# Two-bank order of TensorE's products in a graph-network kernel: first layer, and the second way's second layer

## The chip, the cores and the metric

The kernel runs on one core of one Trainium2 chip. The metric is device microseconds of the whole program, the median of three runs. One further execution was profiled; every duration below comes from it.

## The reference, cut to what matters

A graph with 3,125 nodes of 128 features and 53,125 edges passes through two blocks, each followed by a residual addition and a layer norm. The first block is where the change lies. For every edge an MLP of three layers (384 to 256 to 256 to 128) runs twice, once on (from, to, edge) and once on (to, from, edge), and the results are summed at the target node:

```
def _prop_once(node_states, f_idx, t_idx, edge_features, w1, b1, w2, b2, w3, b3):
    edge_inputs = jnp.concatenate([node_states[f_idx], node_states[t_idx], edge_features], axis=1)
    x = relu(edge_inputs @ w1.T + b1)
    x = relu(x @ w2.T + b2)
    return segment_sum(x @ w3.T + b3, t_idx)
agg = _prop_once(x, src, dst, ...) + _prop_once(x, dst, src, ...)
```

Three GRU cells then use `agg`; the second block is three layers of neighbour sums with a two-layer MLP each.

## The kernel before, in words

The edges are cut into G = 104 groups of GE = 512. `edge_stage` handles one group per turn; `gru_stage` and `sum_stage` follow it. Within `edge_stage` each engine has a `turn(g, ...)` of its own, and the order of its work is written out by hand. The engines meet only at semaphores (`pe.wait_ge(s_he, ...)` and the like). PSUM has eight banks of 128x512 fp32, used by number. Products are made in fp32r with each operand split into a high and a low part, so a product with a 128-wide contraction is three matmuls: high x high, low x high, high x low.

TensorE's turn for group g (L1370) is, in this order:

- `upright(g, 0)` (matmuls at L1329 and L1333): the first way's second layer for the first half of the edges, into bank 6.
- `turn_sd(g + 1)` (L1231, L1310, L1311) and `pairs_of(g)` (L1345): node features of the next group, and edge counts of this one.
- `upright(g, 1)` (L1329, L1333): the other half of the edges, into bank 7.
- `turn_e(g + 1)` (L1231): four 128x128 transposes of the next group's edge features.
- `second(g, 2)` and `second(g, 3)` (L1283): the second way's second layer. Each is six matmuls of 512 columns, the first into bank 6, the other into bank 7.
- `first(g + 1)` (L1270): the first layer of the next group, 18 matmuls of 512 columns. For f = 0 and 1 it makes a shared part (six matmuls, bank 2 + 2f, signalled by `s_p`) and a part whose sign differs between the ways (three matmuls, bank 3 + 2f, signalled by `s_q`).
- `third(1)` (L1293) and `total(g)` (L1361, L1366): the third layer of the second way, and the sums at the nodes.

ScalarE's turn (L707) has in this order: a copy (L624), `upright(g, 0)` (L675, reads bank 6 into `he`), the cast L629, `upright(g, 1)` (L675, reads bank 7 into `he` and raises `s_he` to 2g + 2), the cast L637, `second(g, 2)` and `second(g, 3)` (L667, which read banks 6 and 7 after `s_l2`), the cast L643, in three turns of four a `clear` (L704), then `first(g + 1)`: `shared(0)` (L648, waits for `s_p`), `hidden(0, 0)` (L653), `shared(1)`, and three more `hidden`; then `results` (L682, the tile `es`) and `sums` (L698).

VectorE's `ways(g + 1)` (both at L898, rest at L902) turns the first layer's two parts into `hpre` and `h1l`. It waits for the output of L648 and for `s_q`. Eight times in the whole run a turn ends with `wrap` (L1036, L1038).

`second(g, 2)` writes over bank 6 and `second(g, 3)` over bank 7, so each must wait until ScalarE's L675 has read what `upright` left there. In the kernel before, the first waits for `s_he` at 2g + 1 and the second for 2g + 2.

Of the kernel before, what the change touches and what calls it, by code (L numbers as in the profile page):

```python
# [34 lines left out]
HB = H // P  # L35
# [3 lines left out]
GE = K * P  # L39
# [54 lines left out]
def edge_stage(nc, block, seam, a, adj_flat, tables, along, degrees, npairs, aggw, later, taken, tabs):  # L94

    ctx = ExitStack()
    with ctx:
        def sb(name, shape, dt=fp32):
            return ctx.enter_context(nc.sbuf_tensor(name, shape, dt))

        sem = seam.sem
        bank = seam.bank
# [4 lines left out]
        w1h = sb("w1h", [P, HB, 3, P], f32r)  # L107
        w1l = sb("w1l", [P, HB, 3, P], f32r)
# [31 lines left out]
        sdl = sb("sdl", [P, 3, GE], f32r)  # L140
# [23 lines left out]
        sdh = sb("sdh", [P, 3, GE], f32r)  # L164
# [79 lines left out]
        s_lo = sem("s_lo")  # L244
# [4 lines left out]
        s_p = sem("s_p")  # L249
        s_q = sem("s_q")  # L250
# [4 lines left out]
        s_l2 = sem("s_l2")  # L255
        s_h2 = sem("s_h2")
        s_l3 = sem("s_l3")
        s_he = sem("s_he")
# [970 lines left out]
        def _(pe):  # L1229
            def transpose(out, in_, n):  # L1230
                return nc.tensor.transpose(out, in_, ident[0:n, 0:n])  # L1231
# [3 lines left out]
            for s in range(2):  # L1235
                for k in range(K):
                    last = transpose(bank[s][:, k * G:(k + 1) * G],
                                     rows_f[:, s, :].rearrange("g (p k) -> g k p", k=K)[:, k, :], G)
# [9 lines left out]
            for f in range(HB):  # L1248
                for k in range(HB):
                    last = transpose(bank[4][:, (k * HB + f) * P:(k * HB + f + 1) * P],  # L1250
                                     w2n[:, f, k * P:(k + 1) * P], P)
            last.then_inc(s_wT, 1)
            for k in range(HB):
                last = transpose(bank[5][:, k * P:(k + 1) * P], w3n[k], P)
# [4 lines left out]
            def first(g, start=False, pairs=False):  # L1259
                if not start:  # L1260
                    pe.wait_ge(s_hp, g * 4)
                for f in range(HB):
                    if pairs and f == 1:
                        pe.wait_ge(s_acc, g * 2)
                    for bk, signal, js in ((2, s_p, (0, 2)), (3, s_q, (1,))):
                        parts = [(w, j, x) for j in js for w, x in ((w1h, sdh), (w1h, sdl), (w1l, sdh))]
                        for q, (w, j, x) in enumerate(parts):
                            if f == 0 and j == 2 and q == 3:
                                pe.wait_ge(s_lo, g * 2 + 2)
                            last = nc.tensor.matmul(bank[bk + 2 * f][:, :], w[:, f, j, :], x[:, j, :],  # L1270
                                                    start=(q == 0), stop=(q == len(parts) - 1))
                        last.then_inc(signal, 1)

            PARTS2 = [(w, k, h) for k in range(HB) for w, h in ((w2h, "h"), (w2h, "l"), (w2l, "h"))]

            def units_of(h, way, k, lo, hi):
                return h1h[:, way, k, lo:hi] if h == "h" else h1l[:, k, way, lo:hi]

            def second(g, n):

                way, f = divmod(n, HB)
                for q, (w, k, h) in enumerate(PARTS2):
                    last = nc.tensor.matmul(bank[6 + f][:, :], w[:, k, f, :], units_of(h, way, k, 0, GE),  # L1283
                                            start=(q == 0), stop=(q == len(PARTS2) - 1))
                last.then_inc(s_l2, 1)
# [13 lines left out]
            def windowed():  # L1299
                def turn_sd(g, par, turns, start=False):  # L1300
                    if not start:
                        pe.wait_ge(s_agg, g - 1)
                        pe.wait_ge(s_out, g - 1)
                    pe.wait_ge(s_x[par], turns * (K * 16) + K * 16)
                    for k in range(K):
                        last = transpose(bank[0][:, k * P:(k + 1) * P], xg[par][:, k, :], P)
                    last.then_inc(s_sdT, 1)
                    pe.wait_ge(s_hot, g + 1)
                    pe.wait_ge(s_xl, g + 1)
                    nc.tensor.matmul(bank[1][:, :], xwh[0:SPAN, :], hot[0:SPAN, :], start=True, stop=False)  # L1310
                    nc.tensor.matmul(bank[1][:, :], xwl[0:SPAN, :], hot[0:SPAN, :], start=False, stop=True).then_inc(s_sdT, 1)  # L1311

                def turn_e(g, par, turns, extra=0):
                    pe.wait_ge(s_xs, g + 1)
                    pe.wait_ge(s_ef[par], turns * 16 + (16 + extra))
                    for k in range(K):
                        last = transpose(bank[0][:, k * P:(k + 1) * P], ef[par][:, k, :], P)
                    last.then_inc(s_eT, 1)

                def upright(g, n):  # L1320

                    if n == 0:
                        pe.wait_ge(s_h1l, g * 4 + 4)
                    if not (isinstance(g, int) and g == 0):
                        if n == 0:
                            pe.wait_ge(s_h2, g * 2 - 1)
                        else:
                            pe.wait_ge(s_es, g)
                    nc.tensor.matmul(bank[6 + n][:, :], ones_r[:, :], b2hl[:, :, :].rearrange("p t u -> p (t u)"),  # L1329
                                     start=True, stop=False)  # L1330
                    for t in range(2 * n, 2 * n + 2):
                        for q, (w, k, h) in enumerate(PARTS2):
                            last = nc.tensor.matmul(bank[6 + n][:, t % 2 * H:(t % 2 + 1) * H],  # L1333
                                                    units_of(h, 0, k, t * P, (t + 1) * P),
                                                    w[:, k, :, :].rearrange("p f m -> p (f m)"),
                                                    start=False,
                                                    stop=(q == len(PARTS2) - 1 and t % 2 == 1))
                    last.then_inc(s_l2, 1)

                def pairs_of(g):  # L1340

                    pe.wait_ge(s_ah, g + 1)
                    for half in range(2):
                        for t in range(2):
                            last = nc.tensor.matmul(bank[4 + half][:, 0:WIDER], rowhot[:, half * 2 + t, :],  # L1345
                                                    colhot[:, half * 2 + t, :], start=(t == 0), stop=(t == 1))
                        last.then_inc(s_aT, 1)

                def pair_keys():
                    pe.wait_ge(s_spots, 1)  # L1350
                    for j in range(2):
                        for t in range(K):
                            last = transpose(bank[4 + j][:, t * G:(t + 1) * G],
                                             outb[j][0:G, t, :], G)
                    last.then_inc(s_akT, 1)
# [14 lines left out]
                def turn(g, par, turns, ahead=2, extra=0):  # L1370
                    begin = isinstance(g, int) and g == 0
                    upright(g, 0)
                    if ahead:
                        turn_sd(g + 1, 1 - par, turns)
                    if begin:
                        pair_keys()
                    else:
                        pairs_of(g)
                    upright(g, 1)
                    if ahead:  # L1380
                        turn_e(g + 1, 1 - par, turns, extra)
                    for n in range(2, 4):
                        pe.wait_ge(s_he, g * 2 + (n - 1))
                        second(g, n)
                    if begin:
                        pairs_of(g)
                    if ahead:
                        pe.wait_ge(s_lo, (g + 1) * 2 + 1)
                        first(g + 1, pairs=True)
                    if not ahead:  # L1390
                        into_each()
                        pe.wait_ge(s_agg, g)
                    pe.wait_ge(s_h2, g * 2 + 2)
                    third(1)
                    total(g, par)
# [28 lines left out]
                turn_e(0, 0, 0)  # L1424
                pe.wait_ge(s_lo, 1)
                first(0, start=True)
                turn(0, 0, 0)
                turn(1, 1, 1)
                with pe.Fori(1, (G - 2) // 2) as i:
                    turn(i * 2, 0, i)  # L1430
                    turn(i * 2 + 1, 1, i + 1)
# [127 lines left out]
class Seam:  # L1559
# [20 lines left out]
    def sem(self, name):  # L1580
        return self.ctx.enter_context(self.nc.semaphore(name))
# [748 lines left out]
```

## Time and profile before

| | |
|---|---|
| median of 3 runs | 2269.28 us (2268.61 to 2270.14) |
| the profiled execution | 2266.19 us |
| its span | 2264.4 us |
| PE (TensorE matmul) busy | 2210.4 us, 98% |
| DVE (VectorE) busy | 1777.3 us, 78% |
| ACT (ScalarE) busy | 1166.0 us, 51% |
| POOL (GpSimd) busy | 1165.7 us, 51% |
| mean granted TensorE clock | 0.995 |

The span runs from the first to the last instruction, and 1.8 us of the execution lie around it. PE's busy time counts a matmul from its start to its modelled end, and neighbours overlap in it. What a matmul costs in a stream is therefore the distance between two starts. A row of the timeline gives start, duration, engine, line, operation and count, and in brackets the idle time before it with the releaser. The edge stage fills the span from 37 to 1836 us.

### The profile page before, as it was taken

What the parts mean: (1) busy time and instruction counts of PE and PEld (TensorE: products, weight loads), DVE (VectorE), ACT (ScalarE), POOL (GpSimd) and SP (SyncE); (2) the same over time, 40 slices, a digit from 0 to 9 for tenths busy, and PEclk for the clock granted to TensorE, in tenths of its full rate; (3) what the DMA queues carried; (4) which work ended last, traced back from release to release, by engine and by line L of the source; (5) the groups of instructions that cost most, each with busy time, mean ns of one, the idle gap of its engine ahead of it and who ended that gap; (6) DMA issues with size and microseconds to landing.
All of it is one profiled execution on the core that took longest, in us unless ns stands there. A gap on an engine that the chain in (4) does not pass through costs nothing.

```text
span 2264.4 us, 39847 instructions
## 1 busy us (share of the span) xinstructions
PE 2210.4 (98%) x13211; PEld 1845.9 (82%) x13211; DVE 1777.3 (78%) x4138; ACT 1166.0 (51%) x2019; POOL 1165.7 (51%) x858
## 2 busy tenths in 40 slices
PE   4999999999999999999999999999999999899998
PEld 3888888888888888888888888888888864587876
DVE  7888898898889889888988988898899836703112
ACT  4555566556565555555655565555565533411122
POOL 2466666666666666666666666666665640001100
PEclk9999999999999999999999999999999999999999
DMA  4357455455445445544544544554454359186965
GB/s 154 68 114 149 92 111 99 90 111 108 92 93 115 93 101 110 100 90 101 108 101 93 116 94 90 116 102 91 100 110 92 58 99 271 57 353 258 397 261 209
DMA packets 242868, 292.67 MB, mean 129 GB/s; under 512 B 126820, under 2 KB 200375, under 8 KB 234704
## 3 DMA queue, kind: packets, MB, share of 16 engines
q1 hardware_dynamic: 169554, 237.15, 33.4%
q0 software_dynamic: 73216, 54.58, 18.9%
q14 instruction: 81, 0.66, 0.1%
q8 instruction: 17, 0.28, 0.1%
HBM read 218.56 MB, written 73.08 MB: 129 GB/s over the span
## 4 chain that ended last, share of the span: by engine, by line
PE 94%; DMA 2%; DVE 2%; issue 1%; POOL 1%; ACT 1%; POOLq 0%; SPq 0%; DVEq 0%; ACTq 0%
PE bank L1270 19%; PE bank L1333 13%; PE bank L1283 12%; PE bank L2229 9%; PE bank L1293 8%; PE bank L1361 8%; PE bank L1366 4%; PE bank L1345 4%; PE bank L1231 4%; PE bank L1329 2%; PE bank L1881 2%; PE bank L1310 2%; PE bank L1889 1%; DMA l_ring<-adj 1%; PE bank L1311 1%
## 5 line engine op out<-in xcount | busy, mean ns | idle before, releaser
L514 POOL DMA_INDIRECT sums<-outb,target x416 | 662.2, 1592 | 551.3 <-ACT outb L698 440.4
L507 POOL DMA_INDIRECT xg<-in_x,gidx x416 | 477.4, 1148 | 150.3 <-issue 141.7
L653 ACT ACTIVATE h1h<-hpre 128x512 fp32r<-128x512 f32 x416 | 257.8, 628 | 131.0 <-DVE hpre L898 130.7
L902 DVE SCALAR_TENSOR_TENSOR h1l<-hpre,h1h 128x512 fp32r<-128x512 f32 x416 | 268.6, 688 | 17.0 <-ACT h1h L653 17.0
L898 DVE TENSOR_TENSOR hpre<-pb,bank 128x512 f32<-128x512 f32 x416 | 265.7, 679 | 4.2 <-ACT pb L648 3.4
L1270 PE MATMUL bank<-sdh,w1h 128*128 128x512 f32 x624 | 246.8, 395 | 3.4 <-DVE sdl L930 2.7
L1270 PE MATMUL bank<-sdh,w1l 128*128 128x512 f32 x624 | 247.7, 397 | 0.0
L1270 PE MATMUL bank<-sdl,w1h 128*128 128x512 f32 x624 | 244.8, 392 | 0.0
L1333 PE MATMUL bank<-w2h,h1l 128*128 128x256 f32 x832 | 234.0, 281 | 0.0
L1333 PE MATMUL bank<-w2l,h1h 128*128 128x256 f32 x832 | 233.6, 281 | 0.0
L1333 PE MATMUL bank<-w2h,h1h 128*128 128x256 f32 x832 | 233.3, 280 | 0.0
L667 ACT ACTIVATE h<-bank,b2c 128x512 f32<-128x512 f32 x208 | 143.6, 691 | 145.7 <-PE bank L1283 145.7
L1293 PEld LDWEIGHTS bank<-w3t,h 128*128 128x128 f32 x1664 | 201.7, 192 | 9.3 <-issue 0.2
L1293 PE MATMUL bank<-w3t,h 128*128 128x128 f32 x1664 | 202.5, 275 | 0.1
L1361 PE MATMUL bank<-into,h 128*128 128x64 f32 x1664 | 197.3, 272 | 0.0
L1361 PEld LDWEIGHTS bank<-into,h 128*128 128x128 f32 x1664 | 194.2, 192 | 0.0
L1283 PE MATMUL bank<-h1h,w2h 128*128 128x512 f32 x416 | 172.2, 414 | 0.0
L1016 DVE TENSOR_SCALAR colhot<-spots,colkey 128x475 bf16<-128x475 f16 x416 | 168.4, 405 | 0.0
L2109 DVE TENSOR_TENSOR l_xl<-l_xb,l_xh 128x128 fp32r<-128x128 f32 (+1 forms) x75 | 21.0, 289 | 185.4 <-ACT l_xh L2054 185.4
L1333 PEld LDWEIGHTS bank<-w2h,h1l 128*128 128x128 f32 x832 | 157.6, 189 | 9.2
L629 ACT CAST sdh<-sd 128x1024 fp32r<-128x1024 f32 x104 | 109.1, 1049 | 107.7 <-DVE sd L921 107.7
L1283 PE MATMUL bank<-h1h,w2l 128*128 128x512 f32 x416 | 163.0, 392 | 0.0
(282 smaller groups left out, 4706.7 us busy)
## 6 DMA issues: line engine op xcount, KB each, us to landing
l_ring<-adj SPq DMA_DIRECT2D x54, 1568.0 KB, 7.7
rowb<-along SPq DMA_DIRECT2D x104, 512.0 KB, 4.3
ef<-in_edge_attr SPq DMA_DIRECT2D x103, 256.0 KB, 2.8
adj<-band SPq DMA_DIRECT2D x46, 480.0 KB
adj<-band SPq DMA_DIRECT2D x23, 540.0 KB
stay<-adj SPq DMA_DIRECT2D x6, 1568.0 KB, 15.0
xg<-in_x,gidx POOLq DMA_INDIRECT x416
sums<-outb,target POOLq DMA_INDIRECT x416, 4.1
```

What stands on the lines that cost most here:

```text
L507: pool.indirect_dma_start(out=to, out_offset=None, in_=a["x"], in_offset=bass.IndirectOffsetOnAxis(ap=ids, axis=0)).then_inc(s_x[par], 16)
L514: pool.indirect_dma_start(out=tables[k % 2], out_offset=bass.IndirectOffsetOnAxis(ap=target[par][:, 1, k:k + 1], axis=0), in_=outb[par][:, ...
L653: nc.scalar.activation(h1h[:, way, f, :], hpre[:, f, way, :], ACT.Relu).then_inc(s_h1, 1)
L898: nc.vector.tensor_tensor(hpre[:, f, way, :], pb[:, f, :], bank[3 + 2 * f][:, :], op).then_inc(s_hp, 1)
L902: nc.vector.scalar_tensor_tensor(out=h1l[:, f, way, :], in0=hpre[:, f, way, :], scalar=0.0, in1=h1h[:, way, f, :].bitcast(fp32), op0=ALU.m ...
L1016: nc.vector.tensor_scalar(colhot[:, t, 0:WIDE], spots[:, 0:WIDE], of(colkey, t), None, ALU.is_equal)
L1270: last = nc.tensor.matmul(bank[bk + 2 * f][:, :], w[:, f, j, :], x[:, j, :], start=(q == 0), stop=(q == len(parts) - 1))
L1283: last = nc.tensor.matmul(bank[6 + f][:, :], w[:, k, f, :], units_of(h, way, k, 0, GE), start=(q == 0), stop=(q == len(PARTS2) - 1))
L1293: last = nc.tensor.matmul(bank[6 + way][:, t * P:(t + 1) * P], h2[:, way, k, t * P:(t + 1) * P], w3t[:, k, :], start=not bias and k == 0, ...
L1333: last = nc.tensor.matmul(bank[6 + n][:, t % 2 * H:(t % 2 + 1) * H], units_of(h, 0, k, t * P, (t + 1) * P), w[:, k, :, :].rearrange("p f m ...
L1361: last = nc.tensor.matmul(bank[0][:, k * SPAN:(k + 1) * SPAN], he[:, t, k * P:(k + 1) * P], into[par][:, t, :], start=(t == 0), stop=(t == ...
L2229: last = nc.tensor.matmul(lane(n)[:, 0:width(n)], part[0:r, :], cols if exact else cols.bitcast(fp32), start=False, stop=end)
```

## The change

In `first` the matmuls of the two parts are interleaved: six that go to banks 2 + 2f and 3 + 2f by turns, then the remaining three of the shared part to bank 2 + 2f. `s_q` is raised after the sixth, `s_p` after the ninth. The wait for `s_lo` (2g + 2) stands ahead of the seventh matmul, where it stood ahead of the fourth. In TensorE's windowed `turn` the two calls of `second` are replaced by one loop of twelve matmuls that go to banks 6 and 7 by turns. One wait, for `s_he` at 2g + 2, stands ahead of all twelve. `s_l2` is raised after the eleventh and after the twelfth; it was raised after the sixth and the twelfth. Number, shapes and operands of the matmuls stay the same.

```diff
--- before.py
+++ after.py
@@ -1262,14 +1262,17 @@
                 for f in range(HB):
                     if pairs and f == 1:
                         pe.wait_ge(s_acc, g * 2)
-                    for bk, signal, js in ((2, s_p, (0, 2)), (3, s_q, (1,))):
-                        parts = [(w, j, x) for j in js for w, x in ((w1h, sdh), (w1h, sdl), (w1l, sdh))]
-                        for q, (w, j, x) in enumerate(parts):
-                            if f == 0 and j == 2 and q == 3:
-                                pe.wait_ge(s_lo, g * 2 + 2)
-                            last = nc.tensor.matmul(bank[bk + 2 * f][:, :], w[:, f, j, :], x[:, j, :],
-                                                    start=(q == 0), stop=(q == len(parts) - 1))
-                        last.then_inc(signal, 1)
+
+                    parts = [(j, w, x) for w, x in ((w1h, sdh), (w1h, sdl), (w1l, sdh)) for j in (0, 1)]
+                    parts += [(2, w, x) for w, x in ((w1h, sdh), (w1h, sdl), (w1l, sdh))]
+                    for q, (j, w, x) in enumerate(parts):
+                        if f == 0 and q == 6:
+                            pe.wait_ge(s_lo, g * 2 + 2)
+                        done = nc.tensor.matmul(bank[(3 if j == 1 else 2) + 2 * f][:, :], w[:, f, j, :], x[:, j, :],
+                                                start=q < 2, stop=q in (5, 8))
+                        if q == 5:
+                            done.then_inc(s_q, 1)
+                    done.then_inc(s_p, 1)
 
             PARTS2 = [(w, k, h) for k in range(HB) for w, h in ((w2h, "h"), (w2h, "l"), (w2l, "h"))]
 
@@ -1379,9 +1382,13 @@
                     upright(g, 1)
                     if ahead:
                         turn_e(g + 1, 1 - par, turns, extra)
-                    for n in range(2, 4):
-                        pe.wait_ge(s_he, g * 2 + (n - 1))
-                        second(g, n)
+                    pe.wait_ge(s_he, g * 2 + 2)
+                    for q, (w, k, h) in enumerate(PARTS2):
+                        for f in range(HB):
+                            last = nc.tensor.matmul(bank[6 + f][:, :], w[:, k, f, :], units_of(h, 1, k, 0, GE),
+                                                    start=(q == 0), stop=(q == len(PARTS2) - 1))
+                            if q == len(PARTS2) - 1:
+                                last.then_inc(s_l2, 1)
                     if begin:
                         pairs_of(g)
                     if ahead:
```

## Rows read from the trace of the kernel before

**Rows 1.** Page: busy time by engine; the chain that ended last, by line.
```profile
PE 2210.4 (98%) x13211; PEld 1845.9 (82%) x13211; DVE 1777.3 (78%) x4138; ACT 1166.0 (51%) x2019; POOL 1165.7 (51%) x858
...
PE bank L1270 19%; PE bank L1333 13%; PE bank L1283 12%; PE bank L2229 9%; PE bank L1293 8%; PE bank L1361 8%; PE bank L1366 4%; PE bank L1345 4%; PE bank L1231 4%; PE bank L1329 2%; PE bank L1881 2%; PE bank L1310 2%; PE bank L1889 1%; DMA
```

**Rows 2.** Waits, PE alone, 100 to 1800 us: us in total, times, longest.
```profile
PE bank L1231 <- DMA xg<-in_x,gidx: 0.6, 2, 0.5
```

**Rows 3.** Chain in order of time, one turn: start, us, what.
```profile
1020.47 0.44 PE bank L1231 x4
1020.90 2.76 PE bank L1283 x12
1023.66 4.16 PE bank L1270 x18
```

**Rows 4.** Timeline at `upright(g, 1)` and `second(g, 2)`, turns at 76, 1020 and 1329 us.
```profile
76.69 0.60 ACT L675 ACTIVATE h<-bank 128x512 f32<-128x512 f32 x1
...
76.85 0.48 PE L1283 MATMUL bank<-h1h,w2h 128*128 128x512 f32 x1
...
1020.19 0.28 PE L1333 MATMUL bank<-w2l,h1h 128*128 128x256 f32 x1
...
1020.66 0.48 PE L1283 MATMUL bank<-h1h,w2h 128*128 128x512 f32 x1
...
1020.50 0.60 ACT L675 ACTIVATE h<-bank 128x512 f32<-128x512 f32 x1
...
1329.59 0.60 ACT L675 ACTIVATE h<-bank 128x512 f32<-128x512 f32 x1 [0.15 <-PE bank L1333]
...
1329.75 0.48 PE L1283 MATMUL bank<-h1h,w2h 128*128 128x512 f32 x1
```

**Rows 5.** Timeline: a wait of PE that did last, turn 0.
```profile
62.44 0.65 DVE L1030 TENSOR_TENSOR band<-band,bank 128x475 f32 x1
...
63.15 0.50 PE L1270 MATMUL bank<-sdh,w1h 128*128 128x512 f32 x1 [0.62 <-DVE band L1030]
```

**Rows 6.** A turn after `wrap` at 1295 us, and how many there are.
```profile
1295.38 0.59 ACT L675 ACTIVATE h<-bank 128x512 f32<-128x512 f32 x1
...
1295.12 0.48 PE L1283 MATMUL bank<-h1h,w2h 128*128 128x512 f32 x1
...
L1036 DVE TENSOR_TENSOR band<-band x8: 646/646/651, 259.7 to 1701.1; 128x475 f32<-128x475 f32 x8
```

**Rows 7.** Timeline, PE: L2229, L1345; last, L1345 grouped: busy, mean ns.
```profile
2002.48 1.66 PE L2229 MATMUL bank<-l_ring,l_xh 128*128 128x512 f32 x7
2003.98 1.66 PE L2229 MATMUL bank<-l_ring,l_xl 128*128 128x512 f32 x7
...
1017.81 1.02 PE L1345 MATMUL bank<-colhot,rowhot 128*128 128x500 bf16 x4
...
L1345 PE MATMUL bank<-colhot,rowhot 128*128 128x500 bf16 x416 | 106.1, 377 | 0.0
```

**Rows 8.** Timeline, one turn: ACT, then DVE and PE behind the first layer.
```profile
1008.22 0.68 ACT L648 ACTIVATE pb<-bank,b1c 128x512 f32<-128x512 f32 x1
...
1013.11 0.57 ACT L682 COPY es<-bank 128x512 f32<-128x512 f32 x1
...
1008.20 0.39 PE L1270 MATMUL bank<-sdh,w1l 128*128 128x512 f32 x1
...
1010.27 0.40 PE L1270 MATMUL bank<-sdh,w1l 128*128 128x512 f32 x1
...
1014.03 1.11 PE L1366 MATMUL bank<-es,same 128*128 128x128 f32 x8
...
1009.22 1.27 DVE L898 TENSOR_TENSOR hpre<-pb,bank 128x512 f32<-128x512 f32 x2
...
1011.26 1.28 DVE L898 TENSOR_TENSOR hpre<-pb,bank 128x512 f32<-128x512 f32 x2
```

## The prediction

> **What bounds the kernel now.** I read the page first. PE is busy for 98% of the span and the chain that ended last runs almost wholly through it; the two line numbers that the change touches, L1270 and L1283, hold 19% and 12% of that chain [rows 1]. The other engines have room. Then the waits of PE in the edge stage: between 100 and 1800 us it waited 0.6 us in total for anybody [rows 2]. So a turn of this stage is the sum of PE's own instructions. A saving on them shortens it, and a wait that PE has to sit out lengthens it, one for one. The chain in order of time gives the pieces of a turn without the overlap of neighbours: the twelve matmuls of `second` last 2.76 us, 230 ns each; the eighteen of `first` 4.16 us, 231 ns each; the four transposes between `upright(g, 1)` and `second` only 0.44 us [rows 3]. A turn lasts 17.15 us, and there are 104.
>
> Times are compared so: my sum is made against the profiled execution (2266.19 us, of it 2264.4 the span). The median of the three runs, 2269.28, is 3.1 us above it, and the same increase is laid on it. A difference under 0.2%, 4.5 us, is about what a measurement of this kernel cannot tell from no change.
>
> **The changed order itself.** Count, shapes and operands stay. What changes is how often a matmul goes to another bank than the one before it. In `first`, 14 of the 17 steps between its matmuls stay in their bank before and 4 after; in `second`, 10 of 11 before and none after. That is 20 steps more per turn into another bank, 2080 in all. Is such a step cheaper? The trace has a stretch where every step is of this kind: the second block's panels (L2229) send seven matmuls to seven banks in rotation, six of 512 columns and one of 64. The seven take 2003.98 - 2002.48 = 1.50 us [rows 7]. Give the 64-column one 0.11 us, what one of the transposes of similar weight load takes (0.44 / 4, [rows 3]), and a 512-column matmul costs (1.50 - 0.11) / 6 = 232 ns. In the same bank it is 230 or 231 [rows 3]. Type and width agree (fp32r, 512). Other things differ (L2229 keeps one weight tile for seven matmuls, and rings are loading beside it), but a saving that belongs to the bank should show there and does not. I take zero.
>
> The bounds of this term: above, 2 ns more on each of 2080 steps, +4 us. Below, the bf16 matmuls of L1345 step (1.02 - 0.38) / 3 = 214 ns for 500 columns (0.38 us being the mean length of one, 377 ns), so 219 ns for 512 [rows 7]: 11.5 ns less on 2080 steps, -24 us. I stay at the L2229 end because type and width are the same there; bf16 shows that the engine can do better with other data, not with other banks, as each pair of those matmuls stays in one bank.
>
> Beside it a page. The Trainium skill (TensorE: Matmul & The Clock Gate, section Back-to-back issue gap) puts the isolated gap at N / 2.4 + 2.5 ns, 216 ns for 512 columns. No row of an fp32r matmul here reaches it. Were the bank the reason for the 14 ns between it and the 230 in the trace, 2080 steps would give back 30 us.
>
> **The wait that moved.** This is the term that counts. Before the change the six matmuls into bank 6 start while ScalarE still reads bank 7; only the second six need that bank, 1.4 us later. After it, the one wait for `s_he` at 2g + 2 stands ahead of the first matmul, and the second matmul needs bank 7 in any case. ScalarE's read of bank 7 (L675) cannot start until `upright(g, 1)` is done, and does so at once: the last L1333 ends at 1020.19 + 0.28 = 1020.47, L675 starts at 1020.50 and takes 0.60 us, to 1021.10 [rows 4]. PE has only its 0.44 us of transposes to put in between, and today starts L1283 at 1020.66 [rows 4]. How fast does PE go on after a wait? In turn 0 one did last: VectorE ends at 62.44 + 0.65 = 63.09, the matmul starts at 63.15, 0.06 later [rows 5]. So the first L1283 would start at 1021.10 + 0.06 = 1021.16 and not at 1020.66: 0.50 us. The turn at 76 us gives 76.69 + 0.60 + 0.06 - 76.85 = 0.50, the one at 1329 us 1329.59 + 0.60 + 0.06 - 1329.75 = 0.50 [rows 4]. They are the first and the last of 18 ordinary turns that I read; all give 0.50 or 0.51. Nothing shifts with it in its favour: transposes and L675 both hang on the same end of `upright(g, 1)`, so the gap reappears in each turn.
>
> Two kinds of turn cost more. After a `wrap`, of which there are eight, VectorE and with it ScalarE's cast are late, and L675 ends at 1295.38 + 0.59 = 1295.97, against a first L1283 at 1295.12: 0.91 us with the release [rows 6]. In the last turn there are no transposes, so nothing covers the 0.44 us that they do elsewhere: 0.50 + 0.44 = 0.94 us. Sum: 95 x 0.50 + 8 x 0.91 + 0.94 = 47.5 + 7.3 + 0.9 = 55.7 us.
>
> What is queued behind the waiting PE: `second`, `first(g + 1)`, `third`, `total`, the whole rest of the turn. It all moves by the same amount.
>
> On one page the Trainium skill speaks against this order: Perfetto Trace Analysis, section Matmuls, has independent groups rotate through the banks so that the emptying of one bank runs beside the next group's matmuls. Before, that is what happens at L675 and bank 6; the trace agrees, L1283 starting at 1020.66 in the midst of L675 [rows 4]. By that rule the time comes out on the same side as mine.
>
> **The signals that moved.** `s_q` comes three matmuls earlier, which releases nobody, since VectorE waits for L648 as well. `s_p` comes three later, 0.69 us. For f = 0 it now falls at the end of the ninth matmul, 1008.20 + 0.39 = 1008.59; L648 ran at 1008.22 [rows 8]. With PE's own 0.50 it starts near 1009.13 and ends near 1009.81. VectorE was busy with other work until 1009.22 [rows 8], and that work hangs on the turn before, so L898 starts 0.62 us later than now, 0.12 more than PE has moved. For f = 1 the signal is the end of the last matmul, 1010.27 + 0.40 + 0.50 = 1011.17; L648 (0.67) ends near 1011.88, L898 starts near 1011.91 instead of 1011.26, a lag of 0.15 against PE. The two L667, now released one matmul apart, end about 0.4 us later against PE; `clear` and the new release of L648 fall together, no more is added. The lag goes down to `es` (L682). Today it ends at 1013.11 + 0.57 = 1013.68 and L1366 starts at 1014.03 [rows 8]: 0.35 us, less 0.06 for the release leaves 0.29. A lag of 0.15 fits in. Cost: nothing; if that cover were gone, the lag would be paid in every turn, 0.15 x 103 = 15 us. The other wait moved in `first` (`s_lo`) stands later than before, so it can only be met sooner.
>
> **Sum.** 55.7 us: the profiled execution would go to 2321.9, the median to 2269.3 + 55.7 = 2325.0.
>
> **The rivals.**
>
> 1. The alternation shortens a matmul, beside the stall. With the bf16 step of 219 ns: 2325 - 24 = 2301. Against it L2229. At the floor of one column per cycle of 2.4 GHz (the mean granted clock is 0.995 of full speed), 213 ns, the 20 changed steps give 17 x 2080 = 36 us: 2289. Chance 0.06.
>
> 2. The other side, not slower: the bank sets the step for all thirty matmuls, also those that stay in their bank, and all fall to that floor. 30 x 104 = 3120 matmuls by 17 ns, 54 us, against 56: 2271, the same. It decides from 16.4 ns per matmul on (51.2 us / 3120), which leaves a step of 214 ns. Against it: no fp32r row is near. Chance 0.02; faster by over 0.2% needs still more, or a stall that is hidden by something I don't see: 0.01 of this.
>
> 3. The first layer's chain on ScalarE and VectorE becomes late. If `s_p` carried its full three matmuls down to `es`, 0.69 - 0.29 = 0.40 us in 103 turns, 41 us: 2366. For it: the chain L648, L898, L653, L902 has little slack at its end. Against it: VectorE's own work covers the first 0.5 us. Chance 0.08, mostly of a part of it.
>
> 4. The change doesn't do what it says: the wait bites only at the first matmul that writes bank 7, so one matmul passes, 0.23 us less in each turn, 24 us: 2301. Against it: the diff puts the wait ahead of the loop. Chance 0.02.
>
> **How the numbers follow.** My forecast keeps 0.82. Its own spread: the release 0.02 us longer or shorter (2 us), steps up to 2 ns longer (+4), a remainder of the lag (+5), and a few ns of gain at each changed step (7 ns is -15). That gives 2310 to 2337, and rivals 1, 3 and 4 lie mostly outside, with 0.16. Slower by over 0.2%: 0.82 + 0.05 + 0.08 + 0.02 = 0.97, the case in rival 1 included; same 0.02; faster 0.01.
>
> **What would show it.** In the profile after: a wait of PE, L1283 for ScalarE's L675, about 104 times and 0.4 to 0.5 us each, where there was none; the turn 17.65 instead of 17.15 us; L1283 x12 and L1270 x18 in the chain still at 230 ns a matmul; both L667 back to back; L1366 without a wait for L682. I am wrong if L1283's wait is missing or covered, if the step within L1270 is 220 ns or less, or if PE waits at L1366 or L1329 too.

## Result, and the profile after

| | before | after |
|---|---|---|
| median | 2268.95 us (4 runs, 2268.54 to 2270.14) | 2327.21 us (4 runs, 2325.58 to 2330.67) |
| ratio, 95% interval | | 1.0263 [1.025, 1.0276] |
| profiled execution, of it the span | 2266.19, 2264.4 us | 2327.14, 2325.4 us |
| PE busy | 2210.4 us, 98% | 2239.8 us, 96% |
| a turn in the edge stage | 17.15 us | 17.68 us |

The change costs 58.3 us, 2.6%. The forecast was 2325.0 us, within 2310 and 2337.

The waits of PE between 100 and 1850 us, to be held against [rows 2] (waiting line and releaser, us in total, times, longest):

```profile
PE bank L1388 <- ACT h L675: 29.0, 98, 0.8
PE bank L1231 <- DMA xg<-in_x,gidx: 0.4, 1, 0.4
```

L1388 is the new loop of twelve matmuls. A wait that did not exist stands in each of the 98 turns of this window, and no other has come. The 29.0 us are less than the loss, because this view counts idle time from the modelled end of the last transpose, which overlaps its successor elsewhere; it shows 0.30 us a turn where the prediction had announced 0.4 to 0.5. The chain in order of time (the chain of work that ended last, followed back from its end) counts without overlap (start, us, what), to be held against [rows 3]:

```profile
1052.08 1.42 PE bank L1336 x12
1053.50 0.02 issue
1053.52 0.60 ACT h L675
1054.12 0.04 issue
1054.17 3.04 PE bank L1388 x12
1057.21 4.16 PE bank L1271 x18
1061.37 1.78 PE bank L1296 x16
1063.15 1.73 PE bank L1364 x16
1064.89 0.95 PE bank L1369 x8
```

The chain now leaves PE once a turn. After the last matmul of `upright(g, 1)` it runs through ScalarE's L675 and comes back; the four transposes are no longer on it. From the end of `upright(g, 1)` to the end of `second` it was 1023.66 - 1020.47 = 3.19 us [rows 3] and is 1057.21 - 1053.50 = 3.71 us: 0.52 more. The eighteen matmuls of `first` last 4.16 us, as before.

The same place in the timeline (start, duration, engine, line, and in brackets the idle time and its releaser), with ScalarE and VectorE behind the first layer, to be held against [rows 4, 8]:

```profile
1053.52 0.60 ACT L675 ACTIVATE h<-bank 128x512 f32<-128x512 f32 x1 [0.15 <-PE bank L1336]
...
1054.17 0.74 PE L1388 MATMUL bank<-h1h,w2h 128*128 128x512 f32 x2 [0.25 <-ACT h L675]
1054.75 0.61 PE L1388 MATMUL bank<-h1l,w2h 128*128 128x512 f32 x2
1055.20 0.62 PE L1388 MATMUL bank<-h1h,w2l 128*128 128x512 f32 x2
1055.66 0.62 PE L1388 MATMUL bank<-h1h,w2h 128*128 128x512 f32 x2
...
1041.50 0.28 DVE L925 TENSOR_TENSOR xwl<-xw,xwh 64x128 fp32r<-64x128 f32 x1
1042.37 1.29 DVE L898 TENSOR_TENSOR hpre<-pb,bank 128x512 f32<-128x512 f32 x2 [0.60 <-ACT pb L648]
...
1046.30 0.57 ACT L682 COPY es<-bank 128x512 f32<-128x512 f32 x1
...
1047.04 1.11 PE L1369 MATMUL bank<-es,same 128*128 128x128 f32 x8
```

L675 ends at 1054.12 and the first pair of matmuls starts 0.05 us later. From then on each pair takes 0.45 to 0.47 us, 230 ns per matmul, with every step into the other bank. VectorE, which was busy almost right up to L898 before (4.2 us of idle time ahead of it in the whole run, now 90.9), is free early and waits 0.60 us for L648. `es` ends at 1046.87 and L1369 starts at 1047.04, 0.17 us behind it.

The turn after a `wrap`:

```profile
273.00 1.05 ACT L629 CAST sdh<-sd 128x1024 fp32r<-128x1024 f32 x1 [1.76 <-DVE sd L921]
273.96 0.59 ACT L675 ACTIVATE h<-bank 128x512 f32<-128x512 f32 x1
...
274.60 0.74 PE L1388 MATMUL bank<-h1h,w2h 128*128 128x512 f32 x2 [0.80 <-ACT h L675]
```

Here ScalarE's cast is late and sets L675. From the starts of `second` in neighbouring turns, the eight turns of this kind are 18.22 or 18.23 us long, 1.07 more than an ordinary turn of before. In the last turn `second` starts 0.88 us later against its neighbour than it did. The sum in the trace: 95 x 0.525 + 8 x 1.07 + 0.88 = 59.3 of the 61.0 us between the two spans. Most of the rest, 1.6 us, lies in turn 0, where TensorE's granted clock differed between the two executions (next view: turn 0 from one start of `second` to the next; after the length come PE's busy time and count, then the granted clock; before, then after).

```profile
56.56:76.85 20.29, 18.47 (x118) 1.00 0.18 48
...
56.53:78.94 22.41, 20.30 (x115) 0.92 0.16 43
```

PE stands idle for 1.2 us in this turn, ahead of its last sums. In the execution of after, the clock then was at its lower level, 1.2 GHz, from 70.4 to 73.7 us (0.50 in that stretch): L1369's eight matmuls last 1.96 us and not the 1.16 of before, and those of L1336 step 0.21 us and not 0.12. The change is not the reason. Of the nine profiled executions in this document, turn 0 has a clock of 0.92 in four, two of them without the stall, and lasts 22.1 to 22.4 us; it has 1.00 in five and lasts 20.3 to 21.3 us. Why the same idle time is followed by the lower clock in only four of them is open.

```profile
70.20 1.96 PE L1369 MATMUL bank<-es,same 128*128 128x128 f32 x8 [1.22 <-ACT es L682]
...
72.60 0.41 PE L1336 MATMUL bank<-w2h,h1l 128*128 128x256 f32 x1
72.81 0.41 PE L1336 MATMUL bank<-w2l,h1h 128*128 128x256 f32 x1
```

### The profile page after: what moved, and what is told of

Same layout as the page of the kernel before. It is cut to its first block, busy times and chain, and to the rows that moved or that the text cites. A ratio compares the mean times of both kernels' runs of the same rounds, so it can differ in the third digit from the quotient of the medians.

```text
span 2325.4 us, 39797 instructions
## 1 busy us (share of the span) xinstructions
PE 2239.8 (96%) x13211; PEld 1850.2 (80%) x13211; DVE 1777.6 (76%) x4138; ACT 1161.4 (50%) x2019; POOL 1179.6 (51%) x858
## 4 chain that ended last, share of the span: by engine, by line
PE 86%; DVE 5%; ACT 5%; issue 2%; DMA 1%; POOL 0%; DVEq 0%; POOLq 0%; SPq 0%; ACTq 0%
PE bank L1271 17%; PE bank L1388 13%; PE bank L1336 11%; PE bank L2236 9%; PE bank L1296 7%; PE bank L1364 7%; PE bank L1369 4%; PE bank L1348 4%; ACT h L675 3%; PE bank L1888 2%; PE bank L1332 2%; PE bank L1231 2%; PE bank L1313 2%; PE bank L1896 1%; PE bank L1314 1%
## 5 line engine op out<-in xcount | busy, mean ns | idle before, releaser
L507 POOL DMA_INDIRECT xg<-in_x,gidx x416 | 490.1, 1178 | 150.6 <-issue 141.6
L898 DVE TENSOR_TENSOR hpre<-pb,bank 128x512 f32<-128x512 f32 x416 | 267.1, 683 | 90.9 <-ACT pb L648 90.9
L667 ACT ACTIVATE h<-bank,b2c 128x512 f32<-128x512 f32 x208 | 131.6, 685 | 252.7 <-PE bank L1388 252.7
L1336 PE MATMUL bank<-w2h,h1l 128*128 128x256 f32 x832 | 233.8, 281 | 0.0
L1336 PE MATMUL bank<-w2l,h1h 128*128 128x256 f32 x832 | 233.8, 281 | 0.0
L1336 PE MATMUL bank<-w2h,h1h 128*128 128x256 f32 x832 | 233.3, 280 | 0.0
L1271 PE MATMUL bank<-sdh,w1h 128*128 128x512 f32 x624 | 214.8, 398 | 3.4 <-DVE sdl L930 2.7
L1271 PE MATMUL bank<-sdh,w1l 128*128 128x512 f32 x624 | 212.0, 394 | 0.0
L1271 PE MATMUL bank<-sdl,w1h 128*128 128x512 f32 x624 | 211.7, 393 | 0.0
L1388 PE MATMUL bank<-h1h,w2h 128*128 128x512 f32 x416 | 141.3, 421 | 30.9 <-ACT h L675 30.9
L1336 PEld LDWEIGHTS bank<-w2h,h1l 128*128 128x128 f32 x832 | 157.5, 189 | 9.1
L1336 PEld LDWEIGHTS bank<-w2h,h1h 128*128 128x128 f32 x832 | 158.6, 191 | 2.4
```

What stands on the lines that cost most here:

```text
L507: pool.indirect_dma_start(out=to, out_offset=None, in_=a["x"], in_offset=bass.IndirectOffsetOnAxis(ap=ids, axis=0)).then_inc(s_x[par], 16)
L898: nc.vector.tensor_tensor(hpre[:, f, way, :], pb[:, f, :], bank[3 + 2 * f][:, :], op).then_inc(s_hp, 1)
L1271: done = nc.tensor.matmul(bank[(3 if j == 1 else 2) + 2 * f][:, :], w[:, f, j, :], x[:, j, :], start=q < 2, stop=q in (5, 8))
```

## Experiments

My theory: the loss is the wait ahead of the twelve matmuls, and its size is L675 less what PE has to do beside it. The steps between banks and the later signals cost nothing. The rivals: the order of banks has a price or a gain of its own, hidden under the wait; and the first layer's later signal takes part in the loss. Times are medians; the ratio is to runs of the kernel before on the same chip, whose median was 2267.86 us for the first four kernels and 2267.03 us for the last three.

**The first layer alone.** The new `first`, the old two calls of `second` (against the changed kernel):

```diff
-                    pe.wait_ge(s_he, g * 2 + 2)
-                    for q, (w, k, h) in enumerate(PARTS2):
-                        for f in range(HB):
-...
+                    for n in range(2, 4):
+                        pe.wait_ge(s_he, g * 2 + (n - 1))
+                        second(g, n)
```

> The changed order in the first layer alone; the second layer as before. If the loss is the wait ahead of the second layer, this one costs nothing: 2267 to 2272 us against 2269 before, steps within L1271 still 230 or 231 ns (18 in 4.16 us), no wait of PE at L1369 for ScalarE. If a step into another bank saved up to 17 ns, hidden so far under the wait, ten more such steps a turn would give 2251. If the later signal of the shared part cost more than its cover, PE would wait ahead of L1369 and the time would rise by up to 15 us.

2269.3 us, ratio 1.0007 [0.9998, 1.0016], no difference that can be told. Its chain:

```profile
1041.01 4.16 PE bank L1271 x18
...
1055.40 2.76 PE bank L1286 x12
```

The ten steps more into another bank leave the eighteen matmuls at 4.16 us. PE has no wait at L1369; its waits between 100 and 1830 us are these two:

```profile
PE bank L1231 <- DMA xg<-in_x,gidx: 1.2, 2, 0.8
PE bank L1271 <- DVE sdl L930: 0.2, 1, 0.2
```

But the cover is thinner than it was. In all twelve turns that I read between 1014 and 1203 us, L1369 starts 0.17 us behind the end of `es`, one like the other. The chain to `es` now hangs on PE's own signal in each turn.

**The second layer alone.** The old `first`, the new loop (against the kernel before):

```diff
-                    for n in range(2, 4):
-                        pe.wait_ge(s_he, g * 2 + (n - 1))
-                        second(g, n)
+                    pe.wait_ge(s_he, g * 2 + 2)
+                    for q, (w, k, h) in enumerate(PARTS2):
+                        for f in range(HB):
...
```

> The changed order in the second way's second layer alone, with its one wait; the first layer as before. If the wait is the loss: all of it is here, 2324 to 2328 us, one wait for L675 in each of 104 turns, a turn of 17.68 us. In the turns after a wrap the stall should be 0.91 us instead of 1.07, as the lag of 0.15 us came from the first layer's signals: about 1 us less in all than the whole change. If the first layer's order had a part in the loss, this one would be clearly faster than 2327.

2323.69 us, ratio 1.0243 [1.0227, 1.0258]. The whole loss, but for a few microseconds, is here. An ordinary turn takes 17.68 or 17.69 us. The turns after a `wrap` take 18.13 or 18.14 us instead of 18.22 or 18.23; I had said 0.16 us less, it is 0.09. So the first layer's signals do lengthen these eight turns, by less than a microsecond in all.

**The wait alone.** The kernel before, with one line moved.

```diff
-                    for n in range(2, 4):
-                        pe.wait_ge(s_he, g * 2 + (n - 1))
-                        second(g, n)
+                    pe.wait_ge(s_he, g * 2 + 2)
+                    for n in range(2, 4):
+                        second(g, n)
```

> The kernel before with one difference: the wait for both halves of he stands ahead of the first of the twelve matmuls. Banks and order are as before. If the wait alone makes the loss: 2324 to 2328 us, the same as with the alternation. If going to another bank at each step saved or cost something in the second layer, this one would differ from the run with the second layer's order alone by 11 steps x 104 x the price: 17 ns would be 19 us.

2325.32 us, ratio 1.0258 [1.0242, 1.0274]. No matmul changes place and the loss is all there. Its waits and chain:

```profile
PE bank L1283 <- ACT h L675: 27.9, 98, 0.7
...
1049.04 0.61 ACT h L675
1049.65 0.04 issue
1049.69 3.03 PE bank L1283 x12
```

The twelve matmuls, six into each bank in a row, last 3.03 us from the release; by turns they last 3.04 (the chain after). Turns are 17.67 to 17.68 us long. The price of alternating is thus 0.01 us for the ten steps more into another bank, about 1 ns each, and the medians of the two runs (2323.69 and 2325.32 us) do not show it.

**Three matmuls ahead of the alternation.** Against the changed kernel: the twelve matmuls begin with three into bank 6, enough work to cover L675. Only the new order and its waits are shown; the loop's old head goes.

```diff
+                    pe.wait_ge(s_he, g * 2 + 1)
+                    order = [(q, 0) for q in range(3)]
+                    order += [(q + 3 * (1 - f), f) for q in range(3) for f in (1, 0)]
+                    order += [(q, 1) for q in range(3, 6)]
+                    for at, (q, f) in enumerate(order):
+                        if at == 3:
+                            pe.wait_ge(s_he, g * 2 + 2)
...
```

> The whole change, but the twelve matmuls begin with three into bank 6 behind the old wait (0.69 us of work), then six by turns, then three into bank 7; the wait for bank 7 stands ahead of the fourth. In an ordinary turn the stall of 0.52 us is then covered. Expected 2269 to 2273 us: nothing in 95 turns, 0.2 to 0.4 us in the eight turns after a wrap, where L675 is late. If alternation as such cost time, the 16 or so steps a turn that are still of that kind would show it here.

2272.07 us, ratio 1.0017 [1.0007, 1.0026]. Nearly all of the loss is gone. In this kernel's trace ordinary turns are back at 17.15 us, and the turns after a `wrap` are 17.53 to 17.67 us long, 0.4 more: 3 of the 4.2 us between the medians. PE's waits between 100 and 1830 us no longer name L675, and the twelve matmuls, seven of whose eleven steps go to another bank, last what they did before:

```profile
PE bank L1231 <- DMA xg<-in_x,gidx: 0.5, 2, 0.3
...
1055.91 2.76 PE bank L1393 x12
```

**One matmul beside L675.** Against the changed kernel: its order stays, with the old place for the first bank's wait.

```diff
-                    pe.wait_ge(s_he, g * 2 + 2)
+                    pe.wait_ge(s_he, g * 2 + 1)
                     for q, (w, k, h) in enumerate(PARTS2):
                         for f in range(HB):
+                            if q == 0 and f == 1:
+                                pe.wait_ge(s_he, g * 2 + 2)
```

> The whole change with the wait split: the first of the twelve matmuls (bank 6) waits for the first half of he only, the second (bank 7) for both. One matmul, 0.23 us, then runs beside L675, and the stall in an ordinary turn is 0.29 to 0.30 us instead of 0.52: 95 x 0.29 + 8 x 0.84 + 0.7, about 35 us, 2303 to 2306 us. If the place of the wait did not matter, 2327 again; if only the wait ahead of the first matmul did, 2269.

2303.49 us, ratio 1.0162 [1.0143, 1.0182]. The turn is 17.45 us, 0.295 above the kernel before, and 18.0 us after a `wrap`. Its chain shows the one matmul that slipped through, from 1056.37 us on; the other eleven go on when L675 is done:

```profile
1056.37 0.23 PE bank L1390
1056.60 0.02 issue
1056.62 2.81 PE bank L1390 x11
```

**No cover.** Against the changed kernel: the transposes moved ahead of `upright(g, 1)`, so that PE has nothing to do beside L675.

```diff
-                    upright(g, 1)
                     if ahead:
                         turn_e(g + 1, 1 - par, turns, extra)
+                    upright(g, 1)
```

> The whole change, and the four transposes of turn_e moved ahead of upright(g, 1), so that nothing stands between it and the wait. They take 0.44 us in the chain. If the loss is L675's length less what PE has to do beside it, the stall grows by 0.44 us in the 95 ordinary turns and not in the eight after a wrap (there ScalarE's cast sets it): 42 us more, 2366 to 2372 us. If the loss were in the alternation or in the signals, this would stay near 2327.

2369.06 us, ratio 1.0452 [1.0432, 1.0472].

```profile
1054.32 0.44 PE bank L1231 x4
1054.76 0.23 PE bank L1332
1054.99 1.42 PE bank L1336 x12
1056.41 0.02 issue
1056.43 0.60 ACT h L675
1057.04 0.04 issue
1057.08 3.03 PE bank L1388 x12
```

The transposes stand on the chain again, and L675 with them. The ordinary turn is 18.11 us, 0.43 more than after the change; the turns after a `wrap` are 18.22, the same as after the change. Both as the theory has it: where the late cast sets the end of L675, it does not matter what PE did before.

**The shared part's signal later still.** On top of the first layer alone.

```diff
                         if q == 5:
                             done.then_inc(s_q, 1)
-                    done.then_inc(s_p, 1)
+                        if f == 1 and q == 2:
+                            done.then_inc(s_p, 1)
+                    if f == 1:
+                        done.then_inc(s_p, 1)
```

> The first layer's changed order alone, with the signal of its first shared part (f = 0) raised three matmuls later still, after the third matmul of f = 1, 0.69 us. By my account of the chain L648, L898, L653, L682 the lag at es becomes about 0.8 us, and the slack before L1369, read as 0.35 to 0.63 us less 0.06 for the release, is used up: PE waits there 0.25 to 0.5 us in most turns, 25 to 55 us in all, 2294 to 2324 us. If the chain has more room than I read, it stays at 2269.

2326.92 us, ratio 1.0266 [1.0246, 1.0285]: more than the upper end of what I expected. The waits of PE, and the timeline in one turn:

```profile
PE bank L1372 <- ACT es L682: 37.3, 98, 0.7
...
1057.18 1.29 DVE L898 TENSOR_TENSOR hpre<-pb,bank 128x512 f32<-128x512 f32 x2 [1.01 <-ACT pb L648]
...
1061.08 0.57 ACT L682 COPY es<-bank 128x512 f32<-128x512 f32 x1
1061.70 1.16 PE L1372 MATMUL bank<-es,same 128*128 128x128 f32 x8 [0.38 <-ACT es L682]
```

The mechanism is the expected one: PE waits ahead of the last sums (here L1372) for `es`. The size was wrong because I took the room from the kernel before, where I had read 0.35 to 0.63 us. With the new order in `first` it is 0.17 us in every turn, less about 0.05 for the release (1061.65 to 1061.70 here). 0.69 - 0.12 = 0.57 us, by 103 turns 59 us; turns are 17.69 to 17.75 us long, and the loss is 60 us. Room that was there by VectorE's own lateness cannot be counted again once the chain starts from another signal.

## Why the prediction was right, step by step

**PE bounds the stage, one for one.** Right. In every kernel the loss comes to what its turns grew by. Without the cover that is 95 x 0.96 + 8 x 1.07 + 0.87 = 100.6 us, against 102.0 between the medians.

**A step into another bank is free.** Right, and taken from the right row. `first` keeps its 4.16 us with ten such steps more, and `second` by turns and in rows differ by 0.01 us behind the same wait. The bf16 end (219 ns) and the floor (213 ns) are both out: in neither order did the eighteen or the twelve average under 230 ns a matmul. The step of 216 ns that the Trainium skill gives (TensorE: Matmul & The Clock Gate, Back-to-back issue gap) is not reached in either order, so the bank is not what keeps fp32r from it. What does is open; I tried nothing on it.

**The wait.** Right in kind and place, sized 0.50 us, measured 0.525. The release took 0.05 us and not 0.06. Behind the wait the first matmul and the third start 1054.75 - 1054.17 = 0.58 us apart. In the kernel before it was 0.54, from 1020.66 [rows 4] to the third one's start:

```profile
1021.20 0.39 PE L1283 MATMUL bank<-h1h,w2l 128*128 128x512 f32 x1
```

That is the missing 0.03. The wait alone, the split wait and the missing cover give 0.52, 0.295 and 0.96 us a turn. They follow one sum: L675's 0.60 us, plus 0.06 for the two releases, plus 0.3 that the twelve take longer in the chain from standstill (3.04 against 2.76; 0.24 of it is that in the kernel before the first one starts at 1020.66, beside the last transposes, and the chain counts it from 1020.90 only [rows 3, 4]), less PE's own work beside L675, which is 0.44, 0.44 + 0.23 and nothing. The rule in the Trainium skill (Perfetto Trace Analysis, Matmuls) that one group's bank be emptied beside the next group's matmuls agrees: the kernel with the wait alone breaks it and loses 2.6%, the kernel with three matmuls ahead of the alternation keeps it and loses 0.2%.

**Turns after a wrap.** Sized 0.91 us, measured 1.07, in eight turns: 1.3 us missing. The step that failed is that I read the end of L675 off the kernel before and did not add the lag of the first layer's chain, which I had worked out as 0.15 a few sentences on. With the old `first` these turns lost 0.98 (second layer alone) and 0.92 (wait alone), so 0.09 us came with the new `first` and 0.06 with the alternating loop; what in the loop does it, its later first `s_l2` perhaps, no run shows. The last turn's term was too large by a little: 0.94 us, from the length of the transposes, and measured 0.88.

**The later signals.** Right in outcome: no wait at L1369 appeared. Less of it was cover than I wrote. I worked from one turn with 0.35 us of room and found 0.29 - 0.15 = 0.14 left; measured 0.17 less the release, 0.12. But turns with 0.6 us of room fell to the same 0.17, so their lag was over 0.4. The turn that I read was not like most others, as the turn three later shows in the kernel before:

```profile
1060.41 1.27 DVE L898 TENSOR_TENSOR hpre<-pb,bank 128x512 f32<-128x512 f32 x2
...
1064.30 0.57 ACT L682 COPY es<-bank 128x512 f32<-128x512 f32 x1
...
1065.49 1.11 PE L1366 MATMUL bank<-es,same 128*128 128x128 f32 x8
```

Here L898 starts 5.08 us ahead of L1366 and `es` is ready 0.62 us before it; in the turn of [rows 8] it is 4.81 and 0.35. After the change L898 starts 4.67 us ahead of L1369, now released by L648. So the lag that VectorE's own work leaves is 0.14 us in the turn that I read, near the predicted 0.12, and 0.41 in this one. Rival 3 was nearer than its 0.08 says: another 0.12 us on this signal and PE would have begun to pay, as the last experiment shows. That nothing was paid is in part luck: the turn I worked from understated both the room and the lag.

**The rivals.** 1 and 2 fall with the 4.16 us. 4 (one matmul passes) is the split wait, 2303.49 us, and its sum of 2301 was good; the change itself does not do it.

Sum of the terms as measured: 95 x 0.525 + 8 x 1.07 + 0.88 = 59.3 us against 55.7 predicted and 58.3 between the medians.

## What to carry to other kernels

Before two accumulation groups are interleaved, look at who still reads their banks: the pair can start only when the later of the two banks is empty, and the matmuls of the first group that used to run beside the emptying of the second bank now run behind it. The price can be read off the trace of before, as the end of the emptying plus the release minus the first start today. Room behind a signal belongs to the signal that ends it now, and has to be worked out anew for each kind of turn when that signal is moved.

## What the runs showed of the hardware

Matmuls that go to two banks by turns and matmuls that stay in one bank step equally, 230 to 231 ns for 512 columns in fp32r, within about 1 ns (the eighteen of `first` in 4.16 us in both orders, the twelve of `second` in 3.04 and 3.03 us behind the same wait). An engine behind PE started 0.02 to 0.03 us after PE's end, PE 0.04 to 0.05 us after ScalarE's. And the granted clock early in the program varied from execution to execution of nearly the same instructions: in turn 0 it was 1.00 in five and 0.92 in four, and at 0.92 the turn was 1.6 to 1.9 us longer than the kernel before's plus the stall.
